# A two-layer language-model tower on one core: other instruction orders and PSUM banks

## The reference

```python
h = LN(word[x] + pos[itok] + type[mask]) * gamma + beta
# block P: Performer attention, 16 heads of 16, 44 random features
q, k, v = heads(LN(h) @ Wq.T + bq), ...            # and Wk, Wv
qp = exp(q.proj - |q|^2/.. - max per row) + 1e-4
kp = exp(k.proj - |k|^2/.. - max per head) + 1e-4
o  = (qp @ (kp.T @ v)) / (qp . sum(kp))
h += relu((o @ Wo.T + bo) @ Wfc.T + bfc)
# block F: nearest two of 32 prototypes choose rank-16 experts
d = sqrt(|x|^2 + |p|^2 - 2 x.p); w = softmax(-d/t); top 2, normalised
h += sum over the two of w * (A[i] @ (B[i] @ x) + bias[i])
# block R: causal attention with rotary positions, 16 heads
h += softmax(mask(rope(Q) @ rope(K).T / 4)) @ V @ Wo
# block M: feed-forward 256 -> 1024 -> 256 with ternary weights
h += relu(x @ q(W1).T + b1) @ q(W2).T + b2
```

## Time and profile before

| | before |
|---|---|
| median of 3 runs | 519.68 us |
| profiled execution | 520.48 us |
| its span in the profile | 518.7 us |
| PE busy | 402.6 us, 78% |
| DVE busy | 361.6 us, 70% |
| ACT busy | 264.7 us, 51% |
| POOL busy | 261.1 us, 50% |
| mean granted TensorE clock | 0.905 of full |
| `qk` (L1200) of tile 0 and of tile 15 start at | 36.9 and 399.0 us |
| last store issued | 516.7 us |

### The profile page before, as it was taken

How to read it: one execution, slowest core, us unless ns; L and a number is a source line. 1 busy time by engine, 2 the same in 40 slices (tenths; PEclk the granted TensorE clock), 3 DMA queues, 4 the chain that set the end, 5 groups by cost and what they waited for, 6 DMA issues and landing times.

```text
span 518.7 us, 11425 instructions
## 1 busy us (share of the span) xinstructions
PE 402.6 (78%) x3795; PEld 263.0 (51%) x3795; DVE 361.6 (70%) x997; ACT 264.7 (51%) x563; POOL 261.1 (50%) x350
## 2 busy tenths in 40 slices
...
GB/s 175 175 64 250 153 39 98 28 102 92 159 69 152 67 148 132 117 157 115 162 133 143 85 162 122 120 125 129 122 143 122 137 94 126 54 143 51 91 104 90
DMA packets 198490, 61.62 MB, mean 119 GB/s; under 512 B 190048, under 2 KB 195840, under 8 KB 198432
## 3 DMA queue, kind: packets, MB, share of 16 engines
...
...
## 4 chain that ended last, share of the span: by engine, by line
issue 27%; POOL 18%; DMA 16%; PE 14%; DVE 10%; SPq 7%; ACT 7%; POOLq 0%; ACTq 0%; DVEq 0%
DMA hgT<-hgs 5%; PE PS L1200 4%; POOL stage_f L541 3%; DMA mT<-stage_r 2%; DMA xTP<-xsP 2%; POOL split L544 2%; POOL emb L476 2%; PE PS L1417 2%; POOL hgs L531 2%; SPq L416 2%; SPq L421 2%; SPq L429 2%; PE PS L1499 2%; SPq L396 1%; DMA rTm<-split 1%
## 5 line engine op out<-in xcount | busy, mean ns | idle before, releaser
L535 POOL TENSOR_TENSOR rstdR<-rstdR,consts 128x1 f32<-128x1 f32 x16 | 8.8, 547 | 90.0 <-DVE rstdR L893 90.0
L920 DVE TENSOR_REDUCE split<-PS 128x16 f16<-128x2048 f32 x16 | 36.7, 2296 | 15.7 <-PE PS L1468 15.7
L1156 ACT ACTIVATE stage_p<-PS 128x1024 f32<-128x1024 f32 x16 | 16.4, 1024 | 57.9 <-PE PS L1487 57.9
L1200 PE MATMUL PS<-wqkT_hi,xTP 128*128 128x512 f16 x64 | 24.5, 426 | 24.0 <-DMA xTP<-xsP 24.0
L1417 PE MATMUL PS<-faT_hi,hgT 128*128 128x256 f16 x128 | 27.5, 300 | 19.3 <-DMA hgT<-hgs 14.7
L997 ACT ACTIVATE ehat<-esum,nmeanE,rstdE 128x256 f32<-128x256 f32 x16 | 9.6, 599 | 55.7 <-DVE nmeanE L723 55.7
L1552 PE MATMUL PS<-w2q,mT 128*128 128x256 f16 x256 | 34.7, 295 | 3.9 <-DMA mT<-stage_r 3.9
L1538 PE MATMUL PS<-w1q,xTM 128*128 128x512 f16 x128 | 32.9, 379 | 0.0
L1210 PE MATMUL PS<-proj_hi,qkT 128*128 128x176 f16 x128 | 25.3, 260 | 9.2 <-ACT va L1064 4.4
L1552 PEld LDWEIGHTS PS<-w2q,mT 128*128 128x128 f16 x256 | 26.9, 106 | 10.4 <-issue 3.2
L541 POOL TENSOR_TENSOR stage_f<-stage_f 128x512 f32<-128x512 f32 x16 | 20.3, 1271 | 16.4 <-DVE stage_f L915 16.0
...
## 6 DMA issues: line engine op xcount, KB each, us to landing
...
rT<-split SPq DMA_TRANSPOSE x32, 3.3
```

Source lines behind the costliest of these rows:

```text
L920: v.tensor_reduce(slots(48)[:, 0:H, 0].rearrange("p (c j) -> p j c", j=4), PS[:, BANK["mk1"]:BANK["mk1"] + 4, :].rearrange("p j (c k) -> p ...
L1200: last = pe.matmul(dst, xT[x][:, xp, :], wp[:, c, :], start=(n == 0), stop=(n == 3 * KC - 1 and bias is None))
```

## The change

All numbers of START, STRETCH and PLACE are new, and so are BANK, the bank numbers of two setup products, and WARM. The calls `free(...)` follow from BANK. The steps, their instructions, buffers and the engines that run them are the same.

```diff
-START = (-2.56349, -1.38567, -0.20596, 0.99134, 2.22478, ...)
+START = (3.65732, 5.86818, 8.01069, 10.23857, 12.4764, ...)
...
 BANK = {
-    "qk": 5, "kmxT": 7, "kbc": 6, "fK": 0, "v": 3, "ctx": 6, "fQ": 2, "o": 0,
-    "of": 3, "Ftr": 1, "prt": 7, "fh": 1, "y": 1, "Rtr": 3, "rqk": 3, "rv": 1,
-    "mk1": 4, "pvx": 4, "pvT": 0, "wo": 2, "m1": 2, "m2": 0,
+    "qk": 7, "kmxT": 2, "kbc": 2, "fK": 0, "v": 7, "ctx": 6, "fQ": 0, "o": 6,
+    "of": 2, "Ftr": 4, "prt": 0, "fh": 2, "y": 7, "Rtr": 2, "rqk": 2, "rv": 2,
+    "mk1": 3, "pvx": 5, "pvT": 1, "wo": 7, "m1": 4, "m2": 2,
 }
...
 WARM = {
-    "prt": {15: 3},
-    "s1": {14: 3, 15: 9},
     "rqk": {15: 3},
-    "s2": {15: 4},
-    "pvx": {15: 3},
-    "m1": {14: 3, 15: 3},
-    "m2": {15: 10},
+    "s1": {15: 3},
+    "mk2": {15: 5},
+    "s2": {15: 2},
+    "pvx": {15: 6},
+    "m2": {13: 2, 15: 10},
+    "m1": {15: 3},
 }
...
                 elif op == "fK":
                     wait(pe, qT_ok, 16 * (t + 1))
                     free("kd_ok", kd_ok, t)
+                    free("nd2_ok", nd2_ok, issued["prt"])
+                    free("gt_ok", gt_ok, 2 * issued["prt"])
+                    free("qd_ok", qd_ok, issued["fQ"])
                     free("ro_ok", ro_ok, issued["pvT"])
-                    free("on_ok", on_ok, issued["o"])
-                    free("ob_ok", ob_ok, issued["m2"])
-                    free("hg_ok", hg_ok, issued["fh"])
-                    free("T_F", T_ok["F"], issued["Ftr"])
-                    free("vr_ok", vr_ok, issued["rv"])
-                    free("hF_ok", hF_ok, issued["y"])
                     features(BANK["fK"], HP // 2).then_inc(fK_ok, 1)
```

More of the change, by code:

```diff
@@ L68 @@
[L68 to L75, removed]
@@ new lines @@
+    "Fhi": (2.38042, 2.38042, 2.38042), "FT": (2.92427, 2.92427, 2.92427), "xsq": (2.45806, 2.45806, 2.45806), "prt": (0.92224, 0.92224, 0.92224),
+    "fh": (1.38802, 1.38802, 1.38802), "nd2": (3.23948, 3.23948, 3.23948), "top": (3.48187, 3.48187, 3.48187), "near": (3.55986, 3.55986, 3.55986),
+    "tix": (3.67189, 3.67189, 3.67189), "tpf": (3.46791, 3.46791, 3.46791), "dist": (1.27396, 1.27396, 1.27396), "gap": (3.99342, 3.99342, 3.99342),
+    "sec": (3.82841, 3.82841, 3.82841), "gt": (4.04301, 4.04301, 4.04301), "ws": (4.33868, 4.33868, 4.33868), "gsh": (3.9547, 3.9547, 3.9547),
@@ L948, in step @@
                         .then_inc(nm_ok["M"], 1)
+                elif op == "ml2":
+                    wait(v, mh2_ok, t + 1)
+                    v.scalar_tensor_tensor(out=ms[:, 1, 512:1024], in0=PS[:, BANK["m1"] + 1, :], scalar=0.0,
+                                           in1=ms[:, 0, 512:1024], op0=ALU.max, op1=ALU.subtract).then_inc(ml2_ok, 1)
                 elif op == "ml1":
@@ L1139, in step @@
                     copy(slots(16), rot[:, :, :]).then_inc(rh1_ok, 1)
+                elif op == "rh3":
+                    wait(a, rot_ok, t + 1)
+                    wait(a, rT2_ok, 16 * t)
+                    copy(slots(48)[:, H:, :], rot[:, H:, :]).then_inc(rh3_ok, 1)
                 elif op == "rh2":
@@ L1144, in step @@
                     copy(slots(0)[:, 0:H, :], rot[:, 0:H, :]).then_inc(rh2_ok, 1)
-                elif op == "rh3":
-                    wait(a, rot_ok, t + 1)
-                    wait(a, rT2_ok, 16 * t)
-                    copy(slots(48)[:, H:, :], rot[:, H:, :]).then_inc(rh3_ok, 1)
                 elif op == "vr":
@@ L1180, in step @@
                     copy(xs["M"][:, 0:D], xn["M"][:, :]).then_inc(hi_ok["M"], 1)
+                elif op == "mh2":
+                    wait(a, m1_ok, t + 1)
+                    wait(a, mT_ok, 16 * t)
+                    a.activation(ms[:, 0, 512:1024], PS[:, BANK["m1"] + 1, :], ACT.Relu).then_inc(mh2_ok, 1)
                 elif op == "mh1":
@@ L1184, in step @@
                     a.activation(ms[:, 0, 0:512], PS[:, BANK["m1"] + 0, :], ACT.Relu).then_inc(mh1_ok, 1)
-                elif op == "mh2":
-                    wait(a, m1_ok, t + 1)
-                    wait(a, mT_ok, 16 * t)
-                    a.activation(ms[:, 0, 512:1024], PS[:, BANK["m1"] + 1, :], ACT.Relu).then_inc(mh2_ok, 1)
             setup_p()
@@ L1333, in step @@
                     free("ctl_ok", ctl_ok, t)
-                    free("kb_ok", kb_ok, issued["kbc"])
+                    free("on_ok", on_ok, issued["o"])
                     free("ex2_ok", ex2_ok, issued["mk1"])
@@ L1398, in step @@
                     free("hg_ok", hg_ok, t)
-                    free("T_F", T_ok["F"], issued["Ftr"])
+                    free("kb_ok", kb_ok, issued["kbc"])
+                    free("kmr_ok", kmr_ok, issued["kmxT"])
                     free("vr_ok", vr_ok, issued["rv"])
-                    free("hF_ok", hF_ok, issued["y"])
-                    free("kd_ok", kd_ok, issued["fK"])
+                    free("hP_ok", hP_ok, issued["of"])
+                    free("ob_ok", ob_ok, issued["m2"])
+                    free("rope_ok", rope_ok, 3 * issued["rqk"])
+                    free("T_R", T_ok["R"], issued["Rtr"])
                     split_product(PS[:, BANK["fh"], :], "F", "fbT").then_inc(fh_ok, 1)
@@ L1491, in step @@
                     free("oh_ok", oh_ok, t)
-                    free("ex1_ok", ex1_ok, issued["mk1"])
+                    free("ml2_ok", ml2_ok, issued["m1"])
+                    free("ex2_ok", ex2_ok, issued["mk1"])
                     keep_warm("pvx", t)
@@ L1524, in step @@
                     free("ml1_ok", ml1_ok, t)
-                    free("hR_ok", hR_ok, issued["wo"])
-                    free("qd_ok", qd_ok, issued["fQ"])
+                    free("ex1_ok", ex1_ok, issued["mk1"])
+                    free("T_F", T_ok["F"], issued["Ftr"])
                     free("ml2_ok", ml2_ok, t)
-                    free("va_ok", va_ok, issued["v"])
-                    free("rope_ok", rope_ok, 3 * issued["rqk"])
-                    free("T_R", T_ok["R"], issued["Rtr"])
-                    free("hP_ok", hP_ok, issued["of"])
+                    free("ex2_ok", ex2_ok, issued["mk1"])
+                    free("oh_ok", oh_ok, issued["pvx"])
                     keep_warm("m1", t)
```

178 lines of the change are left out of this document (94 added, 84 removed), and 28 rows, old and new, of the table PLACE.

## The result

| | before | after |
|---|---|---|
| median, 10 runs each | 519.77 us | 512.8 us (508.9 to 515.13) |
| ratio | | 0.9872, 95% interval 0.9835 to 0.9909 |
| profiled execution / its span | 520.48 / 518.7 us | 513.47 / 511.7 us |
| first y; y of tiles 1, 13, 15 | 91.5; 118.8, 413.4, 462.3 | 88.5; 118.2, 399.4, 447.4 |
| rotation add (L541) of tiles 1, 13 | 129.5, 423.6 | 131.4, 414.6 |

The change gained 7.0 us, half of the 13.8 forecast: right in direction, short in size. The y product is L1420 now (L1417 before), s1 L1474, s2 L1496, pvx L1509, m2 L1564; DVE, ACT, POOL and SP have their old lines.

A forecast was written before the change was run, and what follows sets the result against it. A ring of waits through rT, hgT and y bounds the periods, TensorE 88% busy. -7.8 - 1.5 - 3.5 - 1.0 = -13.8 against 520.48 gives 506.7, median 506; range 500 to 512, eight in ten 494 to 523.

The forecast's parts named there:

- The steady ring: Twelve middle periods, y of tile 1 to 13: period falls from 24.55 to 23.9 us, -7.8 us in all.
- The 4.7 us between rT and hgT: SP's queue each period: hgT issued right behind the two rT transposes, so the 4.7 us shrink to hgT's own data need.
- The first tiles: Start up to the first y: first transpose goes out up to 6.5 us earlier, of which 1.5 us are gained.
- The wait for qd: First tiles: fK shares bank 0 with fQ and must wait for qd on DVE; 1 to 2 us left.
- The last tiles: Drain: m2 moved into PE's hole gives -3.5 us; wo of tile 14 before s2 of tile 15 gives -1.0.
- The new order puts m2 ahead of the masks and s1, into the hole: PE in the last tiles: at most 5.7 us back, 3.5 taken.
- The four warm-up matmuls more or fewer in the last tiles stand before waits and cost nothing: PE in the last tiles: no cost, or if not, 0.2 us each.
- The clock in the last tiles: y counted at full pace behind a shorter hole; read strictly, y takes 3.0 us and the drain brings 0.5 of 3.5.
- The slower one: Rival: rTm waits in SP's queue behind hgT, xTo, xTr, xTP; period 25.8, +9, 529 us; chance 0.13.
- No difference: Rival: PE and DVE slip as now, clock takes the drain's gain, fK's wait the head's; 519 to 521 us; chance 0.11.

The follow-up runs named there:

- a_sp_old: After, with SP's order of before around the rT transposes (qkT and xTr ahead of hgT, tiles 2 to 13); ratio to before 1.126, 583.0 us.
- m_before_hgT: Before, with only the hgT transpose of tiles 0 to 13 moved on SP directly behind the two rT transposes; ratio to before 1.055, 549.6 us.
- b_gather: Before, with only gathers of tiles 6 to 15 moved on POOL from behind hgs to ahead of norm R's power; ratio 0.986 and 0.983, 510.9 and 511.6 us.
- d_rqk_first: After, with norm R transposes and rqk of tile 15 ahead of masks and s2 of tile 14 on TensorE; ratio to before 1.001, 519.2 us.
- a_gather_back: After, with gathers of tiles 7 to 15 back right behind hgs on POOL, as in before; ratio to before 1.039, 539.1 us.

## Why the prediction came out as it did

- **The steady ring (-7.8): mechanism right, size off.** The new ring runs through rTm, s2, qk, pvx and rqk; a period is 23.6 us (283.2 / 12) against the 23.9 forecast. The forecast had rTm issued as soon as its data are there; it waits 0.6 us on average. The baseline, though, was no steady one: of before's 24.5 per period, two took 27.3 and 27.5 (rotation adds at 273.4, 300.7, 328.2), with hgT 5.7 and 6.6 us under way and y at half pace. The other ten averaged 23.9. Measured at the rotation add the term is -10.9, not the -13.4 that y shows; against those ten it would be 12 x (23.6 - 23.9), some -4, by an estimate. That it did not fall short of the forecast is luck in this sense: before's profile had two slow periods.
- **What the gain hangs on was not in the sum.** The 4.7 us between rT and hgT were taken as SP's order alone. By the runs it is a bundle: qkT's place (a_sp_old, m_before_hgT), and the gather's, which the prediction counted only as 2.3 us of POOL work. Moved alone it gives before 1.4 to 1.7%, 7 to 8 us; the ways from hgT to y shorten by 6 in all, and why the tail is shorter too is open. How the bundle of after divides between the two was not measured.
- **The first tiles (-1.5): measured +1.9 at the rotation add.** `qk` of tile 0 came 6.0 us earlier (30.9 in place of 36.9) and the first y 3.1. Waits of PE ahead of the first y (L1420) and behind it go along with the loss:
```profile
PE PS L1420 <- DVE rope_sin L688: 3.5, 1, 3.5
PE PS L1210 <- DVE qd L764: 3.0, 1, 3.0
PE PS L1200 <- DVE xTR L901: 2.7, 1, 2.7
```
  An earlier first transpose waits for DVE's set-up; before's first y waited for it as well, 4.7 us. The wait for qd was named but priced too low. And y of tiles 1 to 3 takes 2.5 to 2.7 us in after, near half pace, where before has 1.5; the sum had no such term. No run tested the first tiles alone, so how much of the 3.4 us each of these makes is open.
- **The last tiles (-3.5 and -1.0): the step that failed.** "The new order puts m2 ahead of the masks and s1, into the hole" was to bring y earlier, and did: y of tile 14 starts 9.8 us behind the rotation add of tile 13 in place of 16.1. But y is off the ring in the new orders, and the tail, which was to shrink by 4.5, grew by 2.0. It is worse than that: the old orders' tail is 89.7 and 91.4 with only the gather moved, and 91.0 in m_before_hgT, with one or two m2s at half pace in place of before's three. So part of what the earlier trace rows show was an event of that execution and not the order's price; against b_gather's the new tail is 6 to 7 us longer. Of this 2.5 us are the warm-up of pvx and 0.9 pvx itself at half pace. Another 1.8 to 3.4 arise by the rotation add of tile 15 (46.3 us behind that of tile 13, 43.0 and 44.5 in b_gather's two runs), where s2 of tile 14 waits 2.56 us for rTm and the norm R transposes of tile 15, ready since 451.9, stand behind it:
```profile
453.90 0.62 PE L1496 MATMUL PS<-rTm,rT 64*128 64x128 f16 x16 [2.56 <-DMA rTm<-split]
454.46 0.44 PE L1435 MATMUL PS<-ident,xnR 128*128 128x128 f32 x2
```
  Taking them out from behind it (d_rqk_first) did not shorten the way to s2 of tile 15, so this place alone is not the cause.
- **"The four warm-up matmuls more or fewer in the last tiles stand before waits and cost nothing": wrong.** The new banks put the six of pvx behind a wait, and they cost 2.1 to 2.5 us against 0.2 each in the forecast. Their number was read, the wait ahead of them was not.
- **The clock in the last tiles.** y was counted at full pace behind the shortened hole, and ran so: 0.98 us from the first to the last start of its wide matmuls in tiles 14 and 15, where half pace shows 1.9. No m2 is over 1.65 us by the same measure. The half pace came elsewhere: at pvx of tiles 12 and 13, at rqk of tiles 13 and 14, and at rqk and pvx of tile 15, rqk behind an s2 that had waited 2.56 us, pvx behind waits of 2.53 and 2.04. The Trainium skill ("TensorE: Matmul & The Clock Gate", "What's actually happening") has the throttled clock as the resting state that only activity releases. As the prediction read it, y would have been slowed, which this trace does not show (the last waits in front of y of tiles 14 and 15 are 1.25 and 0.3 us, ahead of s1); rqk and pvx behind the longer waits agree with it.
- **The rivals.** The slower one (rTm behind the other transposes on SP) did not come about in after, but a_gather_back shows that its price was real: +4%. "No difference" is what after shows on two other chips, though not by that rival's mechanism: the middle is shorter there too (285.7 and 290.3 us against 294.1), and the tail gives it back (101.0 and 101.3).

The version that beats both is b_gather, one step moved in the old orders: 511.6 us where before and after take 519.8 and 519.9. On the chips where after does well (1 and 3) it was not run.
